# Mamba stage of a four-stage kernel: u = delta·x and the low half of the carries' small matrix moved from GpSimd to VectorE

## The reference

```python
delta = jax.nn.softplus(jnp.einsum('blr,er->ble', delta, dtw) + dtb)
dA = jnp.exp(delta[..., None] * -jnp.exp(a_log))
mi = ALPHA * delta[..., None] * Bm[:, :, None, :] * xb[..., None]

def scan_fn(carry, inp):
    h, v = carry
    dA_t, mi_t, C_t = inp
    v = BETA * v + mi_t
    h = dA_t * h + v
    y_t = jnp.einsum('ben,bn->be', h, C_t)
    return ((h, v), y_t)
```

## Time and profile before

| | us |
|---|---|
| median of 3 runs | 4501.99 |
| lowest and highest | 4496.07, 4504.96 |
| the profiled execution | 4487.59 |
| its span, first to last instruction | 4485.9 |
| DVE's scans in it (line 1019) | 1354.2 |
| POOL's products in it (line 898) | 1205.4 |

### The profile page before, as it was taken

How to read it: one execution, slowest core, us unless ns; L and a number is a source line. 1 busy time by engine, 2 the same in 40 slices (tenths; PEclk the granted TensorE clock), 3 DMA queues, 4 the chain that set the end, 5 groups by cost and what they waited for, 6 DMA issues and landing times. The chain is left out here.

```text
span 4485.9 us, 88366 instructions
## 1 busy us (share of the span) xinstructions
PE 3543.9 (79%) x28412; PEld 2364.3 (53%) x28413; DVE 2774.5 (62%) x4814; ACT 1980.0 (44%) x4446; POOL 2046.1 (46%) x1206
## 2 busy tenths in 40 slices
PE   6888869936898888888856988889888863199980
PEld 4554546614555555555534555555555543188870
DVE  3444432345777777777765777777777767255545
ACT  1212112215666565665625666566565633133320
POOL 0101000014666676666744667676676764500006
PEclk8888878967999999999987999999999985599995
DMA  4000000012223121231211212122121223311113
GB/s 143 0 0 0 0 21 0 0 56 55 59 53 76 49 74 52 52 74 48 74 38 45 69 50 73 51 60 66 51 73 51 62 74 106 141 47 47 49 37 109
DMA packets 152098, 244.93 MB, mean 55 GB/s; under 512 B 25714, under 2 KB 74130, under 8 KB 149012
## 3 DMA queue, kind: packets, MB, share of 16 engines
q1 hardware_dynamic: 142356, 212.69, 17.4%
q0 software_dynamic: 9344, 27.27, 1.8%
HBM read 119.89 MB, written 38.27 MB: 35 GB/s over the span
## 5 line engine op out<-in xcount | busy, mean ns | idle before, releaser
L898 POOL TENSOR_TENSOR m_hc<-m_h,m_Cb 128x1024 f32<-128x1024 f32 x512 | 1205.4, 2355 | 763.5 <-DVE m_h L1019 466.2
L1019 DVE TENSOR_TENSOR_SCAN m_h<-m_dA,m_hlast,m_bank 128x256 f32<-128x256 f32 x2048 | 1354.2, 725 | 140.1 <-PE m_bank L1300 74.0
L1282 PE MATMUL m_bank<-m_hc,ident 128*128 128x512 f32 x2048 | 1207.7, 679 | 148.5 <-POOL m_hc L898 148.3
L1149 ACT ACTIVATE m_dA<-m_delta,m_rate 128x256 f32<-128x256 f32 x2048 | 894.1, 500 | 16.4 <-DVE m_h L1019 15.4
L1298 PEld LDWEIGHTS m_bank<-m_M,m_U 128*128 128x128 bf16 x8192 | 605.0, 101 | 358.3 <-DVE m_h L1019 222.2
L1298 PE MATMUL m_bank<-m_M,m_U 128*128 128x64 bf16 x8192 | 674.9, 197 | 124.5 <-DVE m_h L1019 117.0
L1300 PEld LDWEIGHTS m_bank<-m_M,m_U 112*128 112x128 bf16 x8192 | 578.5, 100 | 204.5 <-issue 172.6
L1300 PE MATMUL m_bank<-m_M,m_U 112*128 112x64 bf16 x8192 | 675.2, 197 | 0.0
L1282 PEld LDWEIGHTS m_bank<-m_hc,ident 128*128 128x128 f32 x2048 | 337.3, 204 | 198.0 <-POOL m_hc L898 164.9
L967 DVE SCALAR_TENSOR_TENSOR m_cv<-m_xpre,m_conv,m_cv 128x256 f32<-128x256 f32 x384 | 273.3, 753 | 22.6 <-ACT m_cv L1087 18.1
L1212 PE MATMUL m_bank<-m_pair,m_in 128*128 128x256 f32 x1024 | 268.7, 389 | 8.2 <-ACT m_cv L1087 4.4
(11 more groups left out here) (260 smaller groups left out, 5594.2 us busy)
## 6 DMA issues: line engine op xcount, KB each, us to landing
m_Cb<-m_c_rows SPq DMA_DIRECT2D x256, 256.0 KB, 3.2
m_M<-m_Mhi SPq DMA_DIRECT2D x128, 256.0 KB, 4.1
m_M<-m_Mlo SPq DMA_DIRECT2D x64, 256.0 KB, 3.9
m_U<-m_Uhi SPq DMA_DIRECT2D x128, 128.0 KB, 3.3
slots_x<-x_res SPq DMA_DIRECT2D x40, 256.0 KB, 3.0
x_x_in<-slots_x SPq DMA_DIRECT2D x40, 256.0 KB, 2.6
slots_y<-x_y POOLq DMA_DIRECT2D x40, 256.0 KB, 2.3
m_U<-m_Ulo SPq DMA_DIRECT2D x64, 128.0 KB, 3.6
```

The lines of the kernel that those rows point to most:

```text
L898: nc.gpsimd.tensor_tensor(hc[:, n % 2], h[:, n % RING], Cb[:, g % 2, n % NG, :].unsqueeze(1).broadcast_to([P, KI, CM]), ALU.mult).then_inc ...
L1019: nc.vector.tensor_tensor_scan(h[:, n % RING, m, :], dA[:, n % RING, m, :], VB[(n % 2) * 2 + g][:, (m % 2) * CM:(m % 2 + 1) * CM], hlast[: ...
L1149: nc.scalar.activation(dA[:, n % RING, m, :], delta[:, par, m, :], ACT.Exp, scale=rate[:, m, n:n + 1]).then_inc(s["da_done"], 1)
L1282: last = nc.tensor.matmul(Y[half][:], net.ident[:], hc[:, n % 2, 2 * half:2 * half + 2, :], start=(n == 0), stop=(n == NS - 1))
```

## The change

The two POOL instructions are taken out of POOL's `head` and put into DVE's: u directly behind the maxima that make delta (in head 27, after a wait on delta's own semaphore), Glo in head 29.

```diff
@@ POOL, head(q, par, at)
                     if at == 25:
                         matrix_low(q, 0)
-                    if at == 27:
-                        pool.wait_ge(s["ghi_done"], 1 + q + 1)
-                        nc.gpsimd.tensor_tensor(Glo[:], Gf[:].rearrange("p j i n -> p j (i n)"), Ghi[:],
-                                                ALU.subtract).then_inc(s["glo_done"], 1)
-                    if at == 28:
-                        pool.wait_ge(s["delta_done"], 1 + q + 1)
-                        nc.gpsimd.tensor_tensor(u[:], delta[:, par], xb[:, par], ALU.mult).then_inc(s["u_done"], 1)
                     if at == 30:
                         matrix_low(q, 1)
@@ DVE, head(q, par, at)
                         last.then_inc(s["delta_done"], 1)
+                        dve.wait_ge(s["delta_done"], 1 + q + 1)
+                        nc.vector.tensor_tensor(u[:], delta[:, par], xb[:, par], ALU.mult).then_inc(s["u_done"], 1)
+                    if at == 29:
+                        dve.wait_ge(s["ghi_done"], 1 + q + 1)
+                        nc.vector.tensor_tensor(Glo[:], Gf[:].rearrange("p j i n -> p j (i n)"), Ghi[:],
+                                                ALU.subtract).then_inc(s["glo_done"], 1)
```

## The result

The changed kernel is slower by 0.31%: the ratio of its time to that of the kernel before is 1.0031 (95% interval 1.002 to 1.0042). Its median over 20 runs is 4499.95 us, that of the kernel before over 20 runs of its own 4489.66 us, which is 12 us under the three runs that the prediction had. One of the changed kernel's 20 runs, a slow one of 5447.88 us, is outside the ratio. So the absolute 4516.6 us was 17 us too high, most of it from that base, while the step itself, about 14 us by the ratio (10.3 by the medians), is close to the +14.6 us of the sum. The profiled execution took 4502.97 us, 15.4 more than the one before.

A forecast was written before the change was run, and what follows sets the result against it. No engine is full; engines waiting for each other in turn set a chunk's length. 24 x 0.69 - 6 x 0.03 - 2 x 0.9 = +14.6 us on 4487.59, against the median 4516.6 us (4511 to 4522); whole range 4486 to 4552.

The forecast's parts named there:

- u on DVE, 1.30 us: On DVE between delta and the scans of state 9, u takes 1.22 us, 1.30 with the wait for delta's semaphore.
- Its way to the transposes, +0.92 us in 24 chunks and -0.03 in 6: On PE, the transposes move +0.92 us where the accumulation takes 2.07 us (24 chunks), -0.03 where 1.12 (6 chunks).
- The second kind: Chunks where PE's accumulation ahead of the transposes runs at clock 0.99 in 1.12 us: 6 of 30, transposes moving -0.03 us.
- How much arrives, 0.69 of 0.92: From the transposes to the chunk's end, the middle between 0.46 and 0.92 us of delay arrives: 0.69.
- the prediction's two cases: PE's clock returning to 1.00 either moves with the work (0.92 us arrives) or stays at its moment (0.46 us).
- Glo, nothing: On DVE, Glo takes 0.29 us plus its wait, hidden by idle time ahead of Ulo and clo: costed at nothing.
- The rival that Glo costs when its cover is gone: With no DVE idle time left ahead of Ulo and clo, Glo costs 1.1 us in 30 chunks: 4549 us, chance 0.04.
- Ahead of the loops, -0.9 us each: Ahead of each layer's loop, delta to transposes shortens by 0 to 1.1 us; -0.9 taken, near the uncovered end.
- No change: Rival: PE's clock is at its upper level during the accumulation in all chunks, -0.03 us each: 4499 us, chance 0.22.
- Slower through the clock by 2 us a chunk: Rival: a second lower clock stretch grows and 15 short chunks become long, 2.1 us each: 4548 us, chance 0.12.
- Faster, through the clock: Rival: PE's lower clock is over when the transposes start, gaining 1.9 us a chunk: 4485 or 4454 us, chance 0.09.
- Faster, as u is ready sooner: Rival: PE's waits for u go, 15.9 us, and 1.8 ahead of the loops: 4484 us, chance 0.05.

The follow-up runs named there:

- u written twice: The changed kernel with u written twice on DVE, one behind the other: 1.0125 to the kernel before.
- the turned order: The changed kernel with PE's transposes of u put ahead of the first half of the accumulation of state 8: 0.9997; with Glo back on POOL: 0.9925.
- the repeat: The changed kernel measured once more on the same chip as later runs, with no edit: 1.0022 to the kernel before.
- the turned kernel with u on POOL: The kernel before, u and Glo on POOL, with PE's transposes of u put ahead of the accumulation: 1.0107.
- the turned kernels with u on DVE: Two runs of the changed kernel with PE's transposes of u ahead of the accumulation: Glo on DVE 0.9997, Glo back on POOL 0.9925.
- the turned one with Glo on DVE: The changed kernel, u and Glo on DVE, with PE's transposes of u put ahead of the accumulation: 0.9997.

## Why the prediction was right

**u on DVE, 1.30 us.** Right. It took 1.23 us and began 0.03 us behind delta, 1.26 in all.

**Its way to the transposes, +0.92 us in 24 chunks and -0.03 in 6.** The mechanism held, the sizes did not. The product is 1.2 us later, PE's wait for u is gone, and the accumulation at the lower clock stands in its place. But the transposes begin before the modelled end of the accumulation (2876.49 against 2874.63 + 2.08 = 2876.71), which the sum left out, so the chunk shown moved by 0.70, not 0.92. The 22 chunks whose accumulation took 2.07 or 2.08 us before moved by 0.63 on average. The second kind is gone: in the changed kernel the accumulation took 2.07 or 2.08 us in all 30 chunks, and the 6 chunks in which it had taken 1.12 moved by +0.71, where -0.03 was forecast (2 more lay between, at 1.75 and 1.88). The prediction saw no reason for more chunks of the second kind, but kept the 6 there were, though it said itself that PE's idle time ahead would grow; whether that idle time lowered the clock in them no run shows. The two errors of size pull against each other: the mean of the 28 chunks is +0.63, that of the forecast 0.73.

**How much arrives, 0.69 of 0.92.** Three quarters were forecast, between half and all; 0.39 of 0.63 reached chi, about 0.6, and stayed to the end of the chunk (+0.38). The granted clock of the stretches above fits the reason given, since the work up to 2879 ran at 0.50 to 0.55 and from there on at 1.00. All chunks together say more. In the 84 chunks of the kernel before, the changed one and u written twice, the time from the transposes to chi is 7.3 us and 0.48 us more for each us of it in which the granted clock is 0.50, within 0.05 us in every chunk. Two chunks of the kernel before and one of the changed kernel, from the start of the transposes to that of chi (columns as in the earlier trace rows):

```profile
1508.56:1516.37 7.81, 7.81 (x78) 4.84 (x79) 5.72 (x9) 4.36 (x14) 7.64 (x6) 0.94 0.52 135
2864.26:2873.38 9.12, 9.12 (x78) 5.77 (x79) 6.02 (x9) 4.47 (x14) 8.72 (x6) 0.79 0.64 150
```

```profile
2876.49:2885.06 8.57, 8.57 (x79) 5.54 (x78) 7.20 (x12) 4.49 (x13) 8.04 (x6) 0.84 0.62 146
```

Before, 3.56 us of this stretch were at 0.50 on average, in the changed kernel 3.12 and with u written twice 2.37. The return to 1.00 came 0.19 and 0.71 us later than before, for transposes that came 0.63 and 1.91 us later: between the prediction's two cases, nearer to the one in which it stays. So less of the work is left at 0.50 the later it starts, and by the 0.48 this makes up 0.21 and another 0.36 us, about what is missing at chi (0.24 and 0.35). This is how the times go together over many chunks; no run took the clock alone as its variable.

**Glo, nothing.** Right in size and cover: 1.01 us, forecast as 0.29 and the wait for the product, 1.1 in all. DVE stood no longer ahead of Ulo and still 1.99 us ahead of clo. With Glo alone on DVE the time did not move. The rule of the Trainium skill ("SBUF — State Buffer", "Who interferes with whom") held on both sides: Glo took 0.28 us ahead of the loop, where POOL was idle, and 1.01 beside a product. The rival that Glo costs when its cover is gone is what the turned order then showed.

**Ahead of the loops, -0.9 us each.** Mis-sized, as the uncovered end was taken for the likelier. In the first layer, POOL, DVE and PE:

```profile
1035.69 2.29 POOL L849 TENSOR_TENSOR m_Mlo<-m_Mf,m_Mhi 128x1024 bf16<-128x1024 f32 x1 [2.04 <-ACT m_Mhi L1129]
```

```profile
1037.36 1.71 DVE L983 TENSOR_TENSOR m_u<-m_delta,m_xb 128x1024 f32<-128x1024 f32 x1
```

```profile
1039.21 1.94 PE L1246 MATMUL m_bank<-ident,m_u 128*128 128x128 f32 x8 [13.08 <-DVE m_u L983]
```

POOL, rid of u, started the second low half of M 4 us sooner against the end of delta than before (1.6 us ahead of it, not 2.4 behind), and it held DVE's u for 0.5 us. From the end of delta (1037.32) to the transposes it is 1.89 us in place of 2.56, 0.67 saved.

**The sum.** 28 chunks at 0.38 are 10.6 us, the two beginnings give 1.3 back, together +9.3 where +14.6 stood. The times give 10.3 us by the medians and 14 by the ratio, in the repeat 10. By the marks the price of the chunks and the gain at the beginnings were both forecast too large, so the closeness to the 14 is in part luck. In the profile of before and of the changed kernel these chunks are, layer by layer:

```profile
1104.35:2216.83 1112.48, 984.87 (x9282) 618.88 (x9282) 850.45 (x1260) 694.33 (x1610) 754.01 (x379) 0.93 0.24 61
2458.00:3575.39 1117.39, 985.38 (x9282) 618.39 (x9282) 854.53 (x1260) 694.67 (x1611) 754.39 (x379) 0.93 0.24 60
```

```profile
1104.98:2228.40 1123.42, 987.50 (x9282) 625.56 (x9282) 876.67 (x1288) 698.34 (x1611) 703.33 (x351) 0.92 0.24 60
2469.89:3586.92 1117.03, 984.05 (x9282) 624.20 (x9282) 876.71 (x1288) 698.27 (x1611) 703.32 (x351) 0.92 0.24 60
```

The whole difference, 10.9 us, is in the first layer here. In the second profile of the changed kernel the two layers were 1117.02 and 1119.94 us, 4.5 and 2.6 more than before. So the split between the layers is of one execution only. Of the 15.4 us between the two profiled executions 4.8 lie outside these chunks, 3.9 of them behind the last logarithm of the second layer, where only the rest of one of the 30 heads stands; why that stretch is longer stays open. DVE's busy time grew by 26 and 22 us, POOL's fell by 51 in each layer, and neither of these sums tells the result: that of 48 us of work added to DVE, and 102 us taken from POOL, 10.6 us of time came out.

**The rivals.** No change: no, since the accumulation ran at the lower clock, 2.07 us, in every chunk. Slower through the clock by 2 us a chunk: not with this change. The second lower stretch that this rival needs lies about 50 us behind the logarithm. From 48 to 60 us behind it the granted clock is 0.86 in some chunks and 0.72 to 0.76 in the others, which were longer before (80.68 us on average in place of 79.06) and in the changed kernel (81.51 in place of 79.05). There were 10 of these in 28 chunks before and 11 in either profile of the changed kernel. Two chunks of before, then one of u written twice:

```profile
2903.01:2915.01 12.00, 8.77 (x50) 5.32 (x51) 8.35 (x14) 5.78 (x11) 7.05 (x3) 0.72 0.06 22
2984.27:2996.27 12.00, 9.86 (x71) 5.93 (x72) 7.18 (x12) 5.99 (x14) 7.06 (x3) 0.86 0.09 24
```

```profile
3030.33:3042.33 12.00, 9.06 (x50) 5.50 (x51) 8.05 (x13) 5.49 (x11) 7.05 (x3) 0.72 0.07 24
```

With u written twice there were 24, and 23 in the turned kernel with u on POOL. So the rival does come with a larger delay, and fits the 0.48 us that u written twice lost behind chi against the changed kernel. In the turned kernels with u on DVE there were 26 as well, though their chunks are shorter, so this stretch alone does not set the length; why it grows was not followed. Faster, through the clock: no, in every chunk of the changed kernel about 2.5 us or more between the transposes and chi were still at 0.50. Faster, as u is ready sooner: no; u was indeed ready sooner, and it took turning PE's order for the path to use it. The advice of the Trainium skill ("GPSIMD Engine Reference", "4.1 Engine selection") thus held for the durations, 2.36 and 1.23 us, and not for the time.

## What to carry to other kernels

Ask of work moved to a faster engine what is queued behind it there: here 1.2 us on DVE delayed a scan, a product on POOL, a matmul on PE, and only then reached the work that wanted u. An input that is ready sooner is worth nothing until its consumer stands first in its own engine's order: u's move alone cost 0.1% with the consumer where it was, and together with the consumer one step ahead it gained 0.75%, though that step without the move cost 1.07%. And an operation that is free under an idle time should be priced again whenever that idle time is taken away.

## What was not expected of the hardware

The price of a delay was not in proportion to it, and went with where PE's granted clock was at 0.50. The first 0.63 us at the transposes came to 0.39 us at chi and 0.38 us a chunk, the next 1.28 us to 0.93 us at chi and 1.41 us a chunk, all by the marks above: a part was made up ahead of chi, where less of the work was left at 0.50, and the second one grew again behind chi, where more chunks had the long second stretch at 0.50. And the moves on SP's queue became a bound as soon as chi came 2.2 us sooner: PE's wait for the carries' moves went from 1.7 us in the changed kernel to 31.1 us in the turned one with Glo on DVE. In the second layer of the kernel before, this wait is 1.8 us, once.
